# A gated attention block with a routed expert layer: rows copied a chunk later, another order at the handover, row loads one tile further ahead

## The chip, the core and the metric

One core of a Trainium2 chip. The metric is the device time of one execution in microseconds; the times shown are a median over several runs. The core has five engines that run their own instruction streams and signal each other by semaphores: PE (matmuls), ACT (activations, which need a function table loaded), DVE (elementwise work, scans, statistics), POOL (elementwise work and the indirect DMAs), and SP, which here only issues DMAs. All tensors are float32.

## The reference

x has 32 sequences of 256 rows of 128 numbers (8192 rows). Cut to what matters:

```
mod = silu(c) @ wmod                       # six vectors for each sequence
h   = layernorm(x) * (1 + ca) + sa
K   = exp(h Wk1 + bk1);  S = cumsum(K * h) / (cumsum(K) + 1e-6)
Q   = sigmoid(h Wq1 + bq1);  O_ar = S * Q
E   = h[1:] - O_ar[:-1];  K2 = sigmoid(0.02 * (h Wk2 + bk2) / sqrt(128))
O_ma = cumsum(K2 * E) * q2(Q)              # the "moving average" part
x1  = x + ga * ((O_ar + O_ma) Wproj + bproj)
z   = layernorm(x1) * (1 + cb) + sb
e   = argmax(z @ centroids.T)              # one of 8 experts for each row
out = x1 + gb * (z + relu(norm_e(z) W1[e] + b1[e]) W2[e] + b2[e])
```

## The kernel before, in words

**Chunk stage.** The rows are taken in 16 chunks of two sequences (512 rows). The loops of all engines run over c, and one pass holds parts of several chunks: x of chunk c+3 is transposed (PE, L806) and scaled on the way out of PSUM ("turned x", ACT `turned_x`, L953); exp, tanh of k2 and tanh of q (ACT L970, L974, L979) and DVE's scans make O_ar and O_ma; PE adds both products into x1's bank (L779, and L796 for the moving average). ACT copies x1 to `rows` (`sum_of`, L925). Of x1 DVE takes statistics, ACT makes rstd (`rstd_of`, L945 and L947, in the loop L1021 and L1031), POOL makes zz (L501), PE transposes it (`turn_z`, L700), ACT scales it ("turned z", `turned_z`, L933), and PE computes the logits from it (L723) and transposes it back (L700). ACT copies that result to `rows` (`rows_of`, L939: "rows copy"). POOL scatters each finished chunk of rows by expert into DRAM (L538, four indirect DMAs a chunk). Ln and Exp use other tables than tanh, so ACT loads a table twice a pass (L960, L965) and once more in the last pass (L996).

The order on each engine is written out by hand. In ACT's pass c, with z = c-3, it is: turned x, `sum_of(c-1)`, `turned_z(z)`, Ln, table, Exp, exp of k, `rows_of(z)`, tanh, tanh. PE's turn of z waits for ACT's turned x, since both use one bank. In the last pass (c = 15) ACT takes x1's copy, then the table load and `rstd_of(13)`, then `turned_z(12)`; PE runs `turn_z(13)` ahead of the last moving-average products.

**Tile stage.** When 10 chunks are scattered and a first plan is made, SP starts to load tiles of 256 rows that belong to one expert: 25 tiles, 0 to 24, the first 13 from the first plan, tile 13 and on only after all chunks are scattered. Then 11 tiles, 25 to 35, follow in blocks of 128 rows with an expert for each (the last has one block). A tile goes: row load (SP), statistics (DVE `tile_stats`, L1141, for tile j+3), rstd (ACT), normalising (DVE L1485), transposing (PE L843), scaling (ACT), hidden matmuls (PE L830, in block tiles L834), relu (ACT, and for the last quarter of a block tile DVE L1494), the second matmul (PE L858), three sums and a product (DVE, last L1706), store (POOL L613).

SP's queue in step i: the W1 load of tile i+1 (waits until tile i-2's hidden matmuls are done), the row load of tile i+3 (waits for the stores' sums `b_u` and POOL's `b_ids` of the tile whose buffer it takes, nine tiles before), and, in the block stage, two W1 loads of tile i+2. In the block stage a row load is two DMAs of 192.5 KB, and W1 two DMAs of 256 KB.

Of the kernel before, what the change touches and what calls it, by code (L numbers as in the profile page):

```python
# [24 lines left out]
def build_block(nc, x, Wq1, bq1, Wk1, bk1, Wk2, bk2, Wproj, bproj, centroids, ln_g, ln_b,  # L25
# [8 lines left out]
    NC = T // CT  # L34
# [34 lines left out]
    with ExitStack() as ctx:  # L69
# [203 lines left out]
        def in_a(c):  # L273
            return 0 <= c < NC

        def in_b(j):
            return 0 <= j < NJ
# [70 lines left out]
        def _(sp):  # L348
# [43 lines left out]
            for c in range(NC + 1):  # L392
                if in_a(c):
                    fill(c)
                m = c + 7
# [21 lines left out]
            for k in range(RR):  # L417
                sp.wait_ge(s_scat[k], 16 * CN * len(range(k, G1 * GT // CN, RR)))
            sp.wait_ge(s_planned, 1)
            for i in range(-3, NJ):  # L420
                w, m = i + 1, i + 3
                if 0 <= w < NF:
                    e = sp.value_load(plan[0:1, w, 0:1], min_val=0, max_val=E - 1)
                    wait(sp, b_l1, FC * (w - WR + 1))
                    sp.dma_start(w1_full[:, w % WR, :], W1[bass.ds(e, 1), :, :].rearrange("o d f -> (o d) f")
                                 ).then_inc(s_w1[w % WR], 16)
                if in_b(m):
                    if m == N1:
                        for k in range(RR):
                            sp.wait_ge(s_scat[k], 16 * CN * (NC // RR))  # L430
                        sp.wait_ge(s_planned, 2)
                    if m == NF:
                        sp.wait_ge(s_planned, 4)
                    if m < IN_X:

                        sp.wait_ge(s_proj, NC - XR + ((m + 1) * FS * RW - 1) // (CN * D) + 1)
                    wait(sp, b_u, m - FR + 1)
                    wait(sp, b_ids, m - FR + 1)
                    if m < NF:
                        r = sp.value_load(plan[0:1, m, 1:2], min_val=0, max_val=E * RS)  # L440
                        sp.dma_start(full(m), rows_dram[bass.ds(r, FT), :]
                                     .rearrange("(s p) w -> p s w", p=P)).then_inc(s_full[m % FR], 16)
                    else:
                        for t in parts(m):
                            r = sp.value_load(plan[0:1, entry(m, t), 1:2], min_val=0, max_val=E * RS)
                            sp.dma_start(full(m)[:, t, :], rows_dram[bass.ds(r, P), :]).then_inc(s_full[m % FR], 16)
                v = i + 2
                if NF <= v < NJ:
                    wait(sp, b_l1, FC * (v - WR + 1))
                    for t in parts(v):  # L450
                        e = sp.value_load(plan[0:1, entry(v, t), 0:1], min_val=0, max_val=E - 1)
                        sp.dma_start(w1_of(v, t), W1[bass.ds(e, 1), :, :].rearrange("o d f -> (o d) f")
                                     ).then_inc(s_w1[v % WR], 16)
# [182 lines left out]
        def _(pe):  # L636
# [120 lines left out]
            for c in range(-3, NC):  # L757
# [29 lines left out]
                    keep_going(8, ps_t)  # L787
                if in_a(q) and q > 0:
                    queries(q)
                if c == NC - 1:  # L790
                    turn_z(NC - 3)
                if in_a(c):
                    pe.wait_ge(s_M, c + 1)
                    for t in range(CN):
                        s, l = t * P // L, t * P % L
                        mm = pe.matmul(ps_proj[:, t * P:(t + 1) * P], Mp[:, c % 2, s, l:l + P], wg[:, CS * c + s, :],  # L796
                                       start=False, stop=(t == CN - 1))
                    mm.then_inc(s_proj, 1)
                if in_a(a):
                    wait(pe, s_hT, 2 * a)  # L800
                    wait(pe, s_h2T, 2 * max(0, z + 1))
                    for t in range(CN):

                        if a == 0 or t == 0:
                            pe.wait_ge(s_xh, CN * a + t + 1 if a == 0 else CN * (a + 1))
                        mm = pe.transpose(ps_t[:, t * P:(t + 1) * P], xh[:, a % 2, t, :], ident[:, :])  # L806
                    mm.then_inc(s_xT, 1)
# [58 lines left out]
            pe.wait_ge(s_experts, 16 * FC)  # L866
            pe.wait_ge(s_planned, 1)

            keep_going(6, ps_q)
            turn_tile(0)  # L870
            logits(NC - 3)
            turn_back(NC - 3)
# [33 lines left out]
        def _(act):  # L906
# [84 lines left out]
            for c in range(-2, NC):  # L991
                n, q, z, y, o = c + 2, c + 1, c - 3, c - 2, c - 1
                i = c + 4
                if c == NC - 1:
                    sum_of(o)
                    act.preload_act_table_set("natural_log_exp_and_others")  # L996
                    rstd_of(NC - 3)
                if in_a(n) and n != 1:
                    turned_x(n)
                if c == -2:  # L1000
# [7 lines left out]
                                   scale=2.0).then_inc(s_abs, 1)  # L1008
                if in_a(o) and c < NC - 1:
                    sum_of(o)  # L1010
                if in_a(z):
                    turned_z(z)
                if in_a(q):
                    logs(q)
                kinds = slice(0 if in_a(i) else 1, 2 if in_a(y) else 1)
# [19 lines left out]
                if c == NC - 1:  # L1035

                    act.wait_ge(s_planned, 1)
                    of_first = [expert_of(act, n) for n in range(2)]
                if in_a(z):
                    rows_of(z)  # L1040
                if c == 9:
                    act.wait_ge(s_parp, 1)
# [39 lines left out]

            of_blocks = []
            act.wait_ge(s_par, 1)
            rstd_of_tile(0)
            turned_z(NC - 3)
            rstd_of_tile(1)
            experts = [norm_of_expert(0)]
            rstd_of(NC - 2)
            sum_of(NC - 1)  # L1090
            experts.append(norm_of_expert(1))
            rows_of(NC - 3)
# [653 lines left out]
```

## Time and profile before

| | us |
|---|---|
| median of 3 runs (lowest, highest) | 332.16 (331.11, 333.01) |
| the profiled execution | 329.52 |
| its span, first to last instruction | 327.7 |
| busy: PE, PE weight loads | 287.7, 233.1 |
| busy: DVE, ACT, POOL | 253.1, 245.9, 235.4 |

Mean granted PE clock 0.978 of 2.4 GHz. In the page's 40 slices PE is at 9 tenths through the tile stage, and ACT and DVE are at 9 tenths through most of the chunk stage. Busy time is an average over stages with different limits: which wait ends last in a stage has to be read from its timeline. In timeline rows the first column is the start in us from the span's start, the second the duration of the (merged) entry; square brackets give the idle time before it and who ended it.

### The profile page before, as it was taken

What the parts mean: (1) busy time and instruction counts of PE and PEld (TensorE: products, weight loads), DVE (VectorE), ACT (ScalarE), POOL (GpSimd) and SP (SyncE); (2) the same over time, 40 slices, a digit from 0 to 9 for tenths busy, and PEclk for the clock granted to TensorE, in tenths of its full rate; (3) what the DMA queues carried; (4) which work ended last, traced back from release to release, by engine and by line L of the source; (5) the groups of instructions that cost most, each with busy time, mean ns of one, the idle gap of its engine ahead of it and who ended that gap; (6) DMA issues with size and microseconds to landing.
All of it is one profiled execution on the core that took longest, in us unless ns stands there. A gap on an engine that the chain in (4) does not pass through costs nothing.

```text
span 327.7 us, 7878 instructions
## 1 busy us (share of the span) xinstructions
PE 287.7 (88%) x1911; PEld 233.1 (71%) x1911; DVE 253.1 (77%) x653; ACT 245.9 (75%) x538; POOL 235.4 (72%) x371
## 2 busy tenths in 40 slices
PE   8777888899989898998899999999999998998920
PEld 7544445666666565665688999999999998988920
DVE  4898998999999998999945577986666656675840
ACT  2878989999999999999667567776777775666500
POOL 7985476578889888888548878788888753545670
PEclk9999999999999999999989999999999999999985
DMA  7332288626479976444568899778787777877100
GB/s 213 99 105 90 72 228 248 161 90 225 137 202 198 253 196 188 100 149 160 177 224 266 235 289 331 252 219 232 217 228 229 208 225 239 233 220 239 34 16 0
DMA packets 49426, 60.84 MB, mean 186 GB/s; under 512 B 5557, under 2 KB 38095, under 8 KB 49379
## 3 DMA queue, kind: packets, MB, share of 16 engines
q1 hardware_dynamic: 42806, 43.11, 48.9%
q0 software_dynamic: 6368, 16.82, 14.0%
q10 hardware_dynamic: 208, 0.41, 0.4%
q8 instruction: 17, 0.28, 0.3%
q14 instruction: 27, 0.22, 0.2%
HBM read 39.90 MB, written 20.87 MB: 185 GB/s over the span
## 4 chain that ended last, share of the span: by engine, by line
PE 51%; ACT 26%; issue 8%; DVE 7%; SPq 3%; DMA 1%; POOL 1%; POOLq 0%; DVEq 0%; ACTq 0%
PE bank L858 17%; PE bank L830 13%; ACT L965 4%; ACT L960 4%; PE bank L834 4%; PE bank L700 3%; ACT shared L953 3%; ACT shared L960 2%; ACT shared L965 2%; ACT h2T L933 2%; PE bank L843 2%; ACT bank L974 2%; PE bank L796 2%; ACT bank L970 2%; ACT bank L979 2%
## 5 line engine op out<-in xcount | busy, mean ns | idle before, releaser
L613 POOL DMA_INDIRECT out_dram<-shared,ids x71 | 72.4, 1020 | 36.1 <-DVE shared L1706 18.3
L538 POOL DMA_INDIRECT expert_rows<-rows,slots x64 | 66.7, 1043 | 15.8 <-issue 15.0
L858 PE MATMUL bank<-w_all,shared 128*128 x568 | 69.3, 275 | 0.1
L858 PEld LDWEIGHTS bank<-w_all,shared 128*128 128x128 f32 x568 | 66.2, 192 | 0.4 <-issue 0.3
L1054 ACT ACTIVATE shared<-bank,par 128x256 f32<-128x256 f32 x100 | 40.9, 472 | 18.3 <-PE bank L830 18.0
L830 PE MATMUL bank<-shared,early 128*128 128x256 f32 x200 | 47.9, 382 | 0.0
L501 POOL TENSOR_SCALAR zz<-rows,negm,rstd 128x128 f32<-128x128 f32 x64 | 32.3, 517 | 18.6 <-ACT rstd L1031 11.0
L830 PEld LDWEIGHTS bank<-shared,early 128*128 128x128 f32 x200 | 36.1, 190 | 4.1
L1511 DVE TENSOR_TENSOR shared<-bank,b_bc 128x256 f32<-128x256 f32 (+1 forms) x42 | 14.7, 366 | 25.9 <-PE bank L858 24.9
L493 POOL TENSOR_SCALAR xh<-x_in,negm,rstd 128x128 f32<-128x128 f32 x64 | 28.8, 461 | 5.3 <-DVE negm L1260 3.9
L1077 ACT ACTIVATE shared<-bank,par 128x256 f32<-128x256 f32 (+1 forms) x46 | 22.7, 515 | 8.7 <-PE bank L843 6.6
L834 PE MATMUL bank<-shared,rows 128*128 128x128 f32 x168 | 22.1, 279 | 3.9 <-DVE shared L1494 3.9
L1061 ACT ACTIVATE shared<-bank,par 128x128 f32<-128x128 f32 x64 | 18.8, 370 | 8.2 <-PE bank L834 8.1
L834 PEld LDWEIGHTS bank<-shared,rows 128*128 128x128 f32 x168 | 20.1, 192 | 5.0 <-DVE shared L1494 5.0
L796 PEld LDWEIGHTS bank<-wg,Mp 128*128 128x128 f32 x128 | 17.6, 200 | 7.2 <-issue 7.2
L965 ACT ACT_TABLE_LOAD x16 | 20.5, 1283 | 0.3
L960 ACT ACT_TABLE_LOAD x16 | 20.5, 1283 | 0.3
L766 PE MATMUL bank<-x_in,ident 128*128 128x512 f32 x32 | 17.1, 615 | 4.1 <-ACT rows L925 3.2
L933 ACT ACTIVATE h2T<-bank,mod 128x256 f32<-128x256 f32 x32 | 16.3, 559 | 5.3 <-PE bank L700 5.3
L700 PE MATMUL bank<-ident,zz 128*128 128x128 f32 x64 | 10.5, 289 | 11.1 <-ACT shared L953 10.3
L1197 DVE TENSOR_TENSOR_SCAN shared<-seq_mask,bank 128x512 f32<-128x512 f32 x16 | 19.4, 1211 | 0.3 <-ACT bank L970 0.3
L1209 DVE TENSOR_TENSOR_SCAN shared<-seq_mask,bank 128x512 f32<-128x512 f32 x16 | 19.3, 1209 | 0.1
(216 smaller groups left out, 659.5 us busy)
## 6 DMA issues: line engine op xcount, KB each, us to landing
early<-in_L_ffn_W_dram SPq DMA_DIRECT2D x25, 256.0 KB
x_in<-expert_rows SPq DMA_DIRECT2D x15, 385.0 KB, 4.7
rows<-in_L_ffn_W_dram SPq DMA_DIRECT2D x21, 256.0 KB
x_in<-in_L_attn_x_dram SPq DMA_DIRECT2D x16, 256.0 KB, 3.4
rows<-gates_rows SPq DMA_DIRECT2D x32, 128.0 KB, 5.4
full<-expert_rows SPq DMA_DIRECT2D x10, 385.0 KB, 4.5
expert_rows<-pad_rows SPq DMA_DIRECT2D x9, 385.0 KB, 8.4
full<-expert_rows SPq DMA_DIRECT2D x11, 192.5 KB, 3.1
```

The lines of the kernel that those rows point to most:

```text
L493: pool.tensor_scalar(xh[:, a % 2, t, :], x_in[:, a % XR, t, :], negm[:, a, 0, t:t + 1], rstd[:, a, 0, t:t + 1], ALU.add, ALU.mult).then_in ...
L501: pool.tensor_scalar(zz[:, y % 2, t, :], rows[:, y % RR, t, W:W + D], negm[:, y + 6, 1, t:t + 1], rstd[:, y + 6, 1, t:t + 1], ALU.add, ALU ...
L538: pool.indirect_dma_start(rows_dram, bass.IndirectOffsetOnAxis(ap=slots[:, c * CN + t:c * CN + t + 1], axis=0), rows[:, c % RR, t, :], Non ...
L613: pool.indirect_dma_start(out_rows, bass.IndirectOffsetOnAxis(ap=ids[:, u % IR, t:t + 1], axis=0), u_sb[:, k, t, :], None, bounds_check=T - 1,
L796: mm = pe.matmul(ps_proj[:, t * P:(t + 1) * P], Mp[:, c % 2, s, l:l + P], wg[:, CS * c + s, :], start=False, stop=(t == CN - 1))
L830: mm = pe.matmul(hidden_at(j, f), w1_of(j, 0)[:, f * P:(f + 1) * P], zT[:, j % 2, :], start=True, stop=True)
L834: mm = pe.matmul(hidden_at(j, f)[:, t * P:(t + 1) * P], w1_of(j, t)[:, f * P:(f + 1) * P], zT[:, j % 2, t * P:(t + 1) * P], start=True, st ...
L858: mm = pe.matmul(out_at(o, t), hid[:, k, f, t * P:(t + 1) * P], of_expert(w2_all, e, f * D, (f + 1) * D), start=(f == 0), stop=(f == FC - 1))
L933: act.activation(h2T[:, z % 2, s * L:(s + 1) * L], src[:, s * L:(s + 1) * L], ACT.Identity, bias=mod[:, 2, z * CS + s:z * CS + s + 1], sca ...
L960: act.activation(lnK[:, q % 2, :, :], Kc[:, :, :], ACT.Ln, scale=LN_SCALE, bias=epsk[:, :]).then_inc(s_ln, 1)
L965: act.activation(lnK[:, q % 2, :, :], lnK[:, q % 2, :, :], ACT.Exp, scale=-1.0, bias=lnbias[:, :]).then_inc(s_R, 1)
L1054: r = act.activation(hid[:, j % 2, f, :], hidden_at(j, f), ACT.Relu, bias=par[:, 2 + f, bass.ds(e, 1)])
```

## The change

On ACT the rows copy of chunk z moves from the end of pass c to the next pass, between x1's copy and the turned z; the copy of chunk 12 stays where it was. In pass 15 the table load and `rstd_of(13)` move behind `turned_z(12)`. After the loop `rstd_of(14)` and the rstd of tiles 0 and 1 come first, then `turned_z(13)`. On PE the last moving-average products come ahead of `turn_z(13)`, and the filler transposes after the loop are four instead of six. SP's row loads run one tile further ahead from step 7 on, with two in step 6.

```diff
@@ sync
+            def rows_in_step(i):
+                ms = (i + 3,) if i < 6 else (i + 3, i + 4) if i == 6 else (i + 4,)
+                return [m for m in ms if in_b(m)]
             for i in range(-3, NJ):
-                w, m = i + 1, i + 3
+                w = i + 1
                 if 0 <= w < NF:
...
-                if in_b(m):
+                for m in rows_in_step(i):
@@ tensor, loop over c
-                if c == NC - 1:
-                    turn_z(NC - 3)
                 if in_a(c):
                     pe.wait_ge(s_M, c + 1)
...
                     mm.then_inc(s_proj, 1)
+                if c == NC - 1:
+                    turn_z(NC - 3)
@@ tensor, after the loop
-            keep_going(6, ps_q)
+            keep_going(4, ps_q)
@@ scalar, loop over c
                 if c == NC - 1:
                     sum_of(o)
-                    act.preload_act_table_set("natural_log_exp_and_others")
-                    rstd_of(NC - 3)
...
+                if in_a(z - 1):
+                    rows_of(z - 1)
                 if in_a(z):
                     turned_z(z)
+                if c == NC - 1:
+                    act.preload_act_table_set("natural_log_exp_and_others")
+                    rstd_of(NC - 3)
...
-                if in_a(z):
+                if c == NC - 1:
                     rows_of(z)
@@ scalar, after the loop
             act.wait_ge(s_par, 1)
+            rstd_of(NC - 2)
             rstd_of_tile(0)
+            rstd_of_tile(1)
             turned_z(NC - 3)
-            rstd_of_tile(1)
             experts = [norm_of_expert(0)]
-            rstd_of(NC - 2)
             sum_of(NC - 1)
```

## Rows read from the trace of the kernel before

**Rows 1.** Timeline, ACT, one chunk of the chunk stage.

```profile
112.13 0.60 ACT L925 ACTIVATE rows<-bank 128x512 f32<-128x512 f32 x1
113.05 1.02 ACT L933 ACTIVATE h2T<-bank,mod 128x256 f32<-128x256 f32 x2 [0.32 <-PE bank L700]
...
118.90 0.59 ACT L939 ACTIVATE rows<-bank 128x512 f32<-128x512 f32 x1
119.38 0.66 ACT L974 ACTIVATE bank<-bank,bias 128x512 f32<-128x512 f32 x1
119.95 0.67 ACT L979 ACTIVATE bank<-bank,bias 128x512 f32<-128x512 f32 x1
120.54 1.02 ACT L953 ACTIVATE shared<-bank,mod 128x256 f32<-128x256 f32 x2
```

**Rows 2.** Timeline, PE, same chunk: first logits weight load, last x transpose.

```profile
114.15 0.19 PEld L723 LDWEIGHTS bank<-centT,h2T 128*128 128x128 f32 x1 [0.23 <-ACT h2T L933]
...
120.23 0.27 PE L806 MATMUL bank<-ident,xh 128*128 128x128 f32 x1
```

**Rows 3.** Timeline, ACT, pass c = 15.

```profile
157.59 0.60 ACT L925 ACTIVATE rows<-bank 128x512 f32<-128x512 f32 x1 [0.23 <-PE bank L796]
158.21 1.28 ACT L996 ACT_TABLE_LOAD   x1
...
159.95 1.00 ACT L933 ACTIVATE h2T<-bank,mod 128x256 f32<-128x256 f32 x2
```

**Rows 4.** Timeline, PE, from pass c = 15 to the first tile.

```profile
158.10 0.63 PE L700 MATMUL bank<-ident,zz 128*128 128x128 f32 x4
...
161.01 1.06 PE L723 MATMUL bank<-centT,h2T 128*128 128x8 f32 x8 [1.09 <-ACT h2T L933]
...
164.48 1.92 PE L796 MATMUL bank<-wg,Mp 128*128 128x128 f32 x8
...
168.66 1.89 PE L830 MATMUL bank<-shared,early 128*128 128x256 f32 x8
```

**Rows 5.** Timeline, POOL (zz of chunks 13 and 14) and DVE, same stretch.

```profile
160.14 1.73 POOL L501 TENSOR_SCALAR zz<-rows,negm,rstd 128x128 f32<-128x128 f32 x4 [2.85 <-ACT rstd L947]
...
161.83 0.67 DVE L1249 SCALAR_TENSOR_TENSOR Mp<-bank,shared 128x512 f32<-128x512 f32 x1
...
168.85 1.74 POOL L501 TENSOR_SCALAR zz<-rows,negm,rstd 128x128 f32<-128x128 f32 x4 [4.31 <-ACT rstd L947]
```

**Rows 6.** Windows: us, busy of PE, PEld, DVE, ACT, POOL (count), clock, DMA, GB/s.

```profile
164.00:166.00 2.00, 2.00 (x12) 2.00 (x11) 0.36 (x2) 1.24 (x4) 0.54 (x2) 0.50 0.80 265
```

**Rows 7.** Windows, hidden matmuls of tile 26 to those of 27.

```profile
270.39:274.18 3.79, 3.79 (x37) 3.79 (x35) 1.47 (x6) 2.66 (x10) 1.49 (x2) 1.00 0.83 239
```

**Rows 8.** Timeline, SP's queue, tail: W1 of tile 32, rows of tile 35.

```profile
291.26 0.34 SPq L452 DMA_DIRECT2D rows<-in_L_ffn_W_dram  x1
...
296.90 0.34 SPq L446 DMA_DIRECT2D full<-expert_rows  x1
```

**Rows 9.** Timeline, DVE, statistics of tile 35.

```profile
301.29 0.43 DVE L1141 BATCH_NORM_STATS2 bbn<-full 128x6 f32<-128x256 f32 x1 [2.01 <-DMA full<-expert_rows]
```

**Rows 10.** Source view of L446, the row blocks' loads: issue to landing.

```profile
DMA to landing us min/median/max: 2.8/3.1/4.4
```

**Rows 11.** Timeline, PE, hidden matmuls of tile 34.

```profile
306.16 1.95 PE L834 MATMUL bank<-shared,rows 128*128 128x128 f32 x16
```

**Rows 12.** Timeline, POOL, first store of tile 32 and the last store.

```profile
310.43 0.99 POOL L613 DMA_INDIRECT out_dram<-shared,ids  x1 [0.16 <-issue]
...
318.35 0.97 POOL L613 DMA_INDIRECT out_dram<-shared,ids  x1 [0.30 <-issue]
```

**Rows 13.** Timeline, SP's queue, row load of tile 13.

```profile
206.83 0.38 SPq L441 DMA_DIRECT2D x_in<-expert_rows  x1
```

**Rows 14.** Waits of SP's queue, 196 to 212 us: total, times, longest.

```profile
SPq L430 <- DMA expert_rows<-rows,slots: 0.6, 1, 0.6
```

**Rows 15.** Timeline, PE, hidden matmuls of tile 11.

```profile
213.98 1.89 PE L830 MATMUL bank<-shared,early 128*128 128x256 f32 x8
```

## The prediction

> **What bounds the kernel now.** I read the chain of waits first. It shows two long stretches. In the chunk stage (about 26 to 158 us) it goes to and fro between PE and ACT once in every chunk. In the tile stage (about 168 us on) it is PE alone, until 274 us, where it hops to DVE, SP's queue and one row load. So I then opened the timelines: one chunk, the handover between the stages, and the tail.
>
> One chunk, ACT [rows 1]: x1's copy (L925) starts at 112.13, the turned z (L933) at 113.05 after 0.32 us of waiting for PE's transposes, the rows copy (L939) at 118.90, the tanh of q (L979) at 119.95, and the next chunk's turned x (L953) at 120.54. PE, same chunk [rows 2]: the logits' weight load waits 0.23 us for ACT's turned z and starts at 114.15, 0.08 us after L933 ends (113.05 + 1.02 = 114.07). From there PE runs without a gap to its last x transpose at 120.23, and L953 starts 0.31 us behind that (0.27 us of matmul and 0.04 of signal). The loop that sets a chunk's time is thus: turned x, z's transposes, turned z, PE's run, turned x. ACT's own path ends in the same moment: L974 to L979 is 0.57, and 119.95 + 0.57 = 120.52 against 120.54. The two tie within 0.02 us. An ACT made shorter gains nothing by itself; a turned z that starts later costs in full.
>
> The handover: ACT copies x1 of chunk 14 at 157.59, loads the table 158.21 to 159.49, and only then turns z of chunk 12, at 159.95 [rows 3]. PE transposed that z at 158.10 and idles 1.09 us before the logits at 161.01. The eight moving-average products of the last chunk start at 164.48 and take 1.92 us; the first tile's hidden matmuls start at 168.66 [rows 4]. Their input was made by DVE by 162.50 (161.83 + 0.67) [rows 5]: they wait only for their place in PE's order. From 164 to 166 us the granted clock is 0.50, the 1.2 GHz level [rows 6].
>
> The tail: an undisturbed tile of blocks is 3.79 us, all of it PE [rows 7]. SP issues four DMAs a tile (two row blocks, two W1 blocks). From the second W1 block of tile 32 (291.26) to the row block of tile 35 (296.90) there are five gaps, 1.13 us each [rows 8], so 4.51 us a tile: SP is slower than PE. DVE then sits 2.01 us for those last rows [rows 9] with relu, sums and the normalising behind it in its order, and PE waits for DVE.
>
> **The rows copy a chunk later (ACT).** Nothing added: 16 copies before and after. From 118.90 it moves behind x1's copy. ACT there has 0.92 us from 112.13 to 113.05. Two copies need 0.50 (L925's 0.60 less an overlap of 0.10, as L939's 0.59 has: 118.90 to 119.38 is 0.48) + 0.48 = 0.98, so the turned z starts at 113.11 instead of 113.05: +0.06 a chunk. The 0.48 saved later is only waiting for PE. Nine chunks (4 to 12, those with a rows copy there and this loop): +0.55 us. Bounds: if ACT and not PE held the loop, the 0.32 of wait goes: 9 x -0.32 = -2.9; if a copy costs 0.17 more than in [rows 1], 9 x 0.16 = +1.5. I take +0.55, since the 0.31 us and the 0.23 us wait [rows 2] both say PE. What waits for the rows copy: PE's turning back (after the logits, over 1 us later) and POOL's scatter, which in POOL's order stands a whole chunk behind the copy even then. Free.
>
> **The handover (ACT, PE, POOL).** After x1's copy at 157.59 come the rows copy (158.09 to 158.67) and z, whose transposes end at 158.73 (158.10 + 0.63): turned z at 158.76 to 159.76. PE's logits can start at 159.92 (161.01 less its idle 1.09). Logits, turning back and the eight first products, at full clock 0.92 + 0.47 + 0.89 (0.11 or 0.12 for each matmul pass), end at 162.20; the moving-average products wait for DVE's 162.50 and take about 0.96 (half of the 1.92 at half clock) to 163.5, against 166.4 before. The table load now starts at 159.78, 1.57 later, so POOL's zz of chunk 13 goes from 160.14 to 161.71 and ends at 163.44 [rows 5]: just in time for PE, which reaches its transposes at 163.5. Behind it POOL idled 4.31 us before zz of chunk 14 [rows 5], so the 1.57 are covered there, and that zz too comes earlier (its rstd is now first after the loop). Then: transposes to 164.15, turned z to 165.2, logits and turning back 1.4 to 166.7, two tile transposes 0.2, hidden matmuls at 166.9. Before: 168.66. Term: -1.75. The two dropped fillers are worth 0.1 each beside a wait. Bounds: 0 (another wait of the same length) and -2.9 (all that the products gain, 166.4 to 163.5). The rstd of tile 1 now stands before the turned z of chunk 13 and waits for row load 1 through DVE's statistics. Queued behind it are that z, the first expert's scaling and the x1 copy, and PE waits for all three; a load that lands after 164.15 would eat into the term, down to the bound of 0.
>
> [Rows 3] show the table load begin 0.02 us after the copy ends and the turned z stand two small activations behind it, with no room for more. The Trainium skill, "ScalarE: Activation LUTs", section "What ACT_TABLE_LOAD costs", counts a drain of about 1.38 us to each load, 2.66 in all; this trace disagrees. By the page, zz of chunk 13 and all behind it would be 1.38 later, and the time 1.38 above what I forecast; I give that 1 in 100, inside case C.
>
> **Row loads one tile further ahead (SP).** No DMA is added; from step 7 each row load is issued a step earlier, with two at step 6. In the tail each row block is issued 4.51 us sooner; DVE's wait was 2.01, so no tile waits for rows. What is late next is W1. The extra row load was issued long before the tail, so W1's second block of tile v keeps its slot: 291.26 for tile 32, 4.51 less for each tile before. Those of 33 and 34 come 1.1 and 2.3 sooner. Their landing is not shown; a row block of 192.5 KB takes 2.8 to 4.4, median 3.1 [rows 10]; for 256 KB I take 3.6. Then hidden 32 starts at max(274.18 + 5 x 3.79 = 293.13, 291.26 + 3.6 = 294.86) = 294.86, and hidden 34 at 294.86 + 7.58 = 302.44 against 306.16 [rows 11]. PE: -3.7. The end hangs on POOL's stores, in one unbroken row from tile 32 (310.43) to the last (318.35), 7.92 us [rows 12]. The first of them stands 4.27 us behind the start of hidden 34, as its sums need that long, so the row moves with PE: 302.44 + 4.27 + 7.92 = 314.63, term -3.7. Bounds: landing 2.8: hidden 34 at 301.64, -4.5; 4.4: 303.24, -2.9; no W1 wait at all: 274.18 + 7 x 3.79 = 300.71, -5.4; and 0 if W1 takes the whole place.
>
> SP passes one danger. The load of tile 13 stands behind a wait for all scatters, over at 206.83 - 0.6 or so [rows 13, 14]. It now stands before W1 of tile 11 (so far ahead of it), which slips to 206.83 + 1.13 = 207.96; that tile's matmuls start at 213.98 [rows 15], a lead of 6.0 against at most 4.4 for a load [rows 10]. Free with 1.6 us to spare. Between steps 13 and 17 the row loads also reach the point where they wait for POOL's ids; W1 slips by up to 3 us of a lead of 9. Free.
>
> **Sum.** +0.55 - 1.75 - 3.7 = -4.9. The profiled execution took 329.52 (span 327.7, 1.8 lie around it), so 324.6; the median shown is 332.16, 2.64 above it, and the same saving gives 327.3.
>
> **Rivals.**
> - A: ACT really holds the chunk loop. For it: the tie of 0.02 us. Against: 0.31 us behind PE's last transpose. -2.9 in place of +0.55: 323.8. Chance 0.11.
> - C: PE's clock falls at the handover anyway. For: it was down at 164 to 166 [rows 6], soon after PE's idle 1.09 us, and PE still has short waits there. Against: that idle goes, and in the chunk stage PE waits each chunk without a fall. The products, transposes and fillers between 162.5 and 164.7 at half speed cost about 1 of the 1.75: 328.3. Chance 0.14. The Trainium skill, "TensorE: Matmul & The Clock Gate", section "Part 1: The HAM clock gate", says the clock follows how busy PE has lately been, which speaks for no fall.
> - W: W1 takes most of the rows' place. At 5.4 us of landing (1.0 above the longest row load) hidden 34 starts at 304.24 and the tail gives -1.9: 329.1. For: SP issues slower than PE eats. Chance 0.14.
> - N: the row loads do not do what they say, since the same 4.51 us of SP a tile remain: only handover and chunks, -1.2: 331.0. Against: their slots move up in a count of issues. Chance 0.05.
> - S, slower than before: SP stands at the scatter wait of tile 13, and W1 of tile 11 comes after PE wants it. Each us that the scatters land later than 206.2 + 1.6 is a us of PE; it decides against the change from 4.9 us beyond that, and with 8 us it is 335.3. Against: [rows 14] show 0.6 us of wait. Chance 0.04.
>
> **Numbers.** The forecast, 327.3, has the remaining 0.52. The range 323.4 to 330.2 holds it with its bounds, C, W and over half of A; left out are N, S and the rest of A. What can be told from no change here is 0.5%, 1.66 us: faster means below 330.5. Faster 0.91 (forecast, A, C, W), same 0.05 (N), slower 0.04 (S).
>
> **What would show it.** In the profile after: from turned z to turned z 0.06 us more a chunk and no wait of ACT before it (A: 0.3 less). The table load behind the turned z of chunk 12; moving-average products of chunk 15 near 163 at clock 1.0, hidden matmuls of tile 0 some 1.75 sooner. W1 of tile 11 behind the load of tile 13 and no PE wait at tile 11. In the tail no DVE wait for row loads; what stands there instead, PE waiting for W1, sizes W. I am wrong if PE's tail tiles stay near 4.5 us, or if a wait of SP reaches PE between 206 and 235 us.

## The result, and the profile after

| | us | ratio to the kernel before, 95% interval |
|---|---|---|
| kernel before, 4 runs | 331.63 (329.99 to 333.01) | |
| changed kernel, 4 runs | 326.03 (324.01 to 327.96) | 0.9885 [0.984, 0.993] |
| third set of runs, below: before, 17 runs | 330.13 | |
| changed kernel there, 6 runs | 327.35 | 0.9884 [0.9827, 0.9941] |

Faster by 1.15% by the ratio, about 3.8 us, with an interval of 2.3 to 5.3 us. The two medians, of four runs each, stand 5.6 us apart in the first pair and, of 17 and 6 runs, 2.8 us in the third set, so these few runs give the gain to a microsecond or two and no better. The forecast was 4.9 less, 327.3; it lies inside the interval. The profiled execution took 325.93, its span is 324.1 (327.7 before) and its mean clock 0.978, as before.

Starts in us, from the timelines of both kernels (each line's difference holds what came before it):

| | before | after | difference |
|---|---|---|---|
| PE transposes z of chunk 12 | 158.10 | 160.31 | +2.21 |
| hidden matmuls of tile 0 | 168.66 | 169.47 | +0.81 |
| of tile 2 | 178.02 | 178.12 | +0.10 |
| of tile 25 | 266.60 | 266.46 | -0.14 |
| of tile 34 | 306.16 | 302.90 | -3.26 |
| end of the span | 327.7 | 324.1 | -3.6 |

Of the +2.21, 1.8 are not the change's: the first chunks start that much later in this execution, in code that the diff leaves alone. The other 0.4 came in between, over the 12 chunks from the turn of z of chunk 0 (46.55 before, 48.36 after). Other profiles show both starts for both kernels (the turn of z of chunk 12 is at 160.45 in a second profile of the kernel before, at 158.38 in a second one of the changed kernel). So lengths are compared here, not positions.

**Chunk loop.** Timeline of ACT in the changed kernel, one chunk (answers [rows 1]; L958 is turned x, L930 x1's copy, L944 the rows copy, L938 turned z):

```profile
122.50 1.02 ACT L958 ACTIVATE shared<-bank,mod 128x256 f32<-128x256 f32 x2 [0.37 <-PE bank L811]
123.41 0.60 ACT L930 ACTIVATE rows<-bank 128x512 f32<-128x512 f32 x1
123.89 0.60 ACT L944 ACTIVATE rows<-bank 128x512 f32<-128x512 f32 x1
124.37 1.04 ACT L938 ACTIVATE h2T<-bank,mod 128x256 f32<-128x256 f32 x2
...
131.84 1.02 ACT L958 ACTIVATE shared<-bank,mod 128x256 f32<-128x256 f32 x2 [0.37 <-PE bank L811]
```

The wait before the turned z is gone, and a wait of 0.37 for PE's x transposes stands before the turned x instead. From turned x to turned x it is 9.34, against 9.32 before. ACT's saving turned into waiting: PE's run holds this loop, with ACT's stretch from turned x to turned z in it.

**Handover.** Timeline of PE in the changed kernel (answers [rows 4]; L705 turns z, L728 logits, L799 moving-average products, L645 fillers, L848 transposes of tile 0, L835 its hidden matmuls):

```profile
160.31 0.66 PE L705 MATMUL bank<-ident,zz 128*128 128x128 f32 x4
...
162.08 1.06 PE L728 MATMUL bank<-centT,h2T 128*128 128x8 f32 x8
...
164.62 1.16 PE L799 MATMUL bank<-wg,Mp 128*128 128x128 f32 x8
165.78 0.66 PE L705 MATMUL bank<-ident,zz 128*128 128x128 f32 x4
166.27 0.60 PE L645 MATMUL bank<-ident 128*128 128x128 f32 x4
167.24 0.44 PE L848 MATMUL bank<-ident,shared 128*128 128x128 f32 x2 [0.37 <-DVE shared L1494]
167.86 1.06 PE L728 MATMUL bank<-centT,h2T 128*128 128x8 f32 x8 [0.18 <-ACT h2T L938]
...
169.47 1.89 PE L835 MATMUL bank<-shared,early 128*128 128x256 f32 x8
```

Windows of the same kernel (us, busy of PE, PEld, DVE, ACT, POOL with counts, granted clock, DMA share, GB/s; answers [rows 6]):

```profile
164.00:166.00 2.00, 1.90 (x15) 1.52 (x14) 1.55 (x4) 0.94 (x4) 1.85 (x5) 1.00 0.85 261
```

What PE waited for in the two short gaps between 164 and 166 us (DVE's input of the moving-average products; POOL's zz of chunk 13):

```profile
163.88 0.68 DVE L1258 SCALAR_TENSOR_TENSOR Mp<-bank,shared 128x512 f32<-128x512 f32 x1
163.98 1.75 POOL L506 TENSOR_SCALAR zz<-rows,negm,rstd 128x128 f32<-128x128 f32 x4 [3.58 <-ACT rstd L952]
```

PE's products start at 164.62, 0.06 behind DVE's end (163.88 + 0.68), and its turn of z of chunk 13 at 165.78, 0.05 behind POOL's (163.98 + 1.75). The idle 1.09 before the logits is gone, and the clock is 1.00 where it was 0.50. From turn to tile 0 it is 9.16 instead of 10.56, from turn to tile 2 17.81 instead of 19.92. ACT shows a new wait (answers [rows 3]; L1020 is the table load):

```profile
161.01 1.02 ACT L938 ACTIVATE h2T<-bank,mod 128x256 f32<-128x256 f32 x2 [0.27 <-PE bank L705]
162.04 1.28 ACT L1020 ACT_TABLE_LOAD   x1
163.34 0.30 ACT L950 ACTIVATE lnv<-bn,epsv 128x4 f32<-128x4 f32 x1
163.67 0.21 ACT L952 ACTIVATE rstd<-lnv 128x4 f32<-128x4 f32 x1
165.03 0.60 ACT L944 ACTIVATE rows<-bank 128x512 f32<-128x512 f32 x1 [1.16 <-issue]
...
166.80 1.00 ACT L938 ACTIVATE h2T<-bank,mod 128x256 f32<-128x256 f32 x2
```

Between 163.88 and 165.03 ACT reads the first two experts from the plan into registers. The last row is the turned z of chunk 13: it has no wait, for ACT comes to it only at 166.80, 0.36 after PE's transposes have ended (165.78 + 0.66 = 166.44). The load starts 0.01 us after the turned z ends (161.01 + 1.02 = 162.03), and the next activation 0.02 after the load. The Trainium skill, "ScalarE: Activation LUTs", section "What ACT_TABLE_LOAD costs", adds a drain of about 1.38 us to a load; this second place shows no room for one either.

**Tail.** Hidden matmuls of tiles 30 to 34, timeline of PE in the changed kernel (answers [rows 11]):

```profile
285.42 2.02 PE L839 MATMUL bank<-shared,rows 128*128 128x128 f32 x16
...
290.26 2.02 PE L839 MATMUL bank<-shared,rows 128*128 128x128 f32 x16 [0.81 <-issue]
...
294.53 2.02 PE L839 MATMUL bank<-shared,rows 128*128 128x128 f32 x16 [0.24 <-issue]
...
299.04 2.02 PE L839 MATMUL bank<-shared,rows 128*128 128x128 f32 x16 [0.48 <-issue]
...
302.90 1.95 PE L839 MATMUL bank<-shared,rows 128*128 128x128 f32 x16
```

SP's queue there (second W1 block of tiles 31, 32 and 33; answers [rows 8]), and the source view of L457, the W1 blocks' loads (its last line; it stands beside [rows 10]):

```profile
286.98 0.34 SPq L457 DMA_DIRECT2D rows<-in_L_ffn_W_dram  x1
...
291.46 0.34 SPq L457 DMA_DIRECT2D rows<-in_L_ffn_W_dram  x1
...
294.89 0.34 SPq L457 DMA_DIRECT2D rows<-in_L_ffn_W_dram  x1
```

```profile
DMA to landing us min/median/max: 2.8/3.0/3.3
```

The hidden matmuls start 3.28, 3.07 and 4.15 us behind the issue of the second W1 block of their tile, after short waits to which the profile gives no releaser ("issue"). The landing is on record for only 7 of the 21 W1 blocks, and the last line is over those 7. One is the second block of tile 32: issued at 291.46 with 2.98 to landing, it was there at 294.44, and PE starts at 294.53. For tile 33 no landing is on record, and 4.15 is longer than any of the 7. That this wait too is W1's is an argument by elimination: the tile's turned rows were ready at 297.75 (ACT, 296.94 + 0.81) and the first relus of tile 32, which free the bank, were done by 297.01 (ACT, 295.86 + 1.15), both long before 299.04. Tiles 25 to 30 pass at 3.79 or 3.80. From tile 25 to 34 it is 36.44 instead of 39.56. DVE's waits for row loads from 264 us on fall from 13.5 us in 9 to 4.0 in 4, and no wait of PE for DVE is left there (3.9 us in 6 before). The last store (answers the second of [rows 12]):

```profile
314.76 0.97 POOL L618 DMA_INDIRECT out_dram<-shared,ids  x1 [0.30 <-issue]
```

It is 3.59 earlier, 0.33 more than the start of tile 34; the stores moved with PE.

### The profile page after: what moved, and what is told of

Its sections match the earlier page's. It is cut to its first block, busy times and chain, and to the rows that moved or that the text cites. A ratio compares the mean times of both kernels' runs of the same rounds, so it can differ in the third digit from the quotient of the medians.

```text
span 324.1 us, 7874 instructions
## 1 busy us (share of the span) xinstructions
PE 286.6 (88%) x1909; PEld 232.0 (72%) x1909; DVE 253.1 (78%) x653; ACT 244.6 (75%) x538; POOL 238.4 (74%) x371
## 4 chain that ended last, share of the span: by engine, by line
PE 56%; POOL 23%; issue 10%; ACT 3%; DMA 3%; DVE 1%; POOLq 1%; ACTq 0%; DVEq 0%
PE bank L863 18%; PE bank L835 14%; POOL expert_rows L543 9%; PE bank L839 6%; POOL xh L498 6%; POOL zz L506 5%; PE bank L848 2%; PE bank L771 2%; PE bank L784 2%; PE bank L705 2%; PE bank L728 2%; PE bank L799 2%; PE bank L759 2%; PE bank L756 2%; PE bank L749 1%
## 5 line engine op out<-in xcount | busy, mean ns | idle before, releaser
L618 POOL DMA_INDIRECT out_dram<-shared,ids x71 | 73.2, 1031 | 31.0 <-issue 12.8
L835 PE MATMUL bank<-shared,early 128*128 128x256 f32 x200 | 47.7, 381 | 0.0
L835 PEld LDWEIGHTS bank<-shared,early 128*128 128x128 f32 x200 | 36.1, 190 | 4.1
L498 POOL TENSOR_SCALAR xh<-x_in,negm,rstd 128x128 f32<-128x128 f32 x64 | 29.5, 472 | 4.3 <-DVE negm L1269 3.9
L839 PE MATMUL bank<-shared,rows 128*128 128x128 f32 x168 | 20.9, 277 | 1.5 <-issue 1.5
L799 PEld LDWEIGHTS bank<-wg,Mp 128*128 128x128 f32 x128 | 16.7, 191 | 7.5 <-issue 7.2
L705 PE MATMUL bank<-ident,zz 128*128 128x128 f32 x64 | 10.1, 280 | 12.1 <-ACT shared L958 10.3
L958 ACT ACTIVATE shared<-bank,mod 128x256 f32<-128x256 f32 x32 | 16.3, 561 | 5.8 <-PE bank L811 5.8
## 6 DMA issues: line engine op xcount, KB each, us to landing
full<-expert_rows SPq DMA_DIRECT2D x11, 192.5 KB, 3.0
```

What stands on the lines that cost most here:

```text
L498: pool.tensor_scalar(xh[:, a % 2, t, :], x_in[:, a % XR, t, :], negm[:, a, 0, t:t + 1], rstd[:, a, 0, t:t + 1], ALU.add, ALU.mult).then_in ...
L618: pool.indirect_dma_start(out_rows, bass.IndirectOffsetOnAxis(ap=ids[:, u % IR, t:t + 1], axis=0), u_sb[:, k, t, :], None, bounds_check=T - 1,
L835: mm = pe.matmul(hidden_at(j, f), w1_of(j, 0)[:, f * P:(f + 1) * P], zT[:, j % 2, :], start=True, stop=True)
L839: mm = pe.matmul(hidden_at(j, f)[:, t * P:(t + 1) * P], w1_of(j, t)[:, f * P:(f + 1) * P], zT[:, j % 2, t * P:(t + 1) * P], start=True, st ...
```

## The experiments

Three sets, each on one chip, every kernel beside the kernel before. The chips differed: the kernel before took 359.72 us (35 runs) in the first set, 366.97 (23 runs) in the second and 330.13 (17 runs) in the third. That matters below.

### One part at a time

`rows_ahead_only` is the kernel before with SP's part of the diff, `handover_only` with ACT's and PE's edits of the last pass and behind the loop, `rows_copy_only` with the moved rows copy, each as in the diff above. `after_again` is the changed kernel.

> The kernel before with SP's row loads one tile further ahead and nothing else. Theory (the tail is set by when SP issues; W1 is late next): hidden matmuls of tile 25 at the same place relative to tile 0, those of tile 34 3.0 to 3.7 us nearer to those of tile 25 than the 39.6 us of before, whole kernel 3.3 us faster (2.5 to 4.0). No DVE wait for row loads over 1.5 us in the tail; PE instead waits a few tenths of a us for W1 in tiles 31 to 33. Rival N (SP spends the same time a tile, so nothing is won): within 0.5 us of before. Rival S: a PE wait at tile 11 or 12, since W1 of tile 11 now stands behind SP's wait for the scatters.

360.02, ratio 0.9964 [0.9911, 1.0017].

> The kernel before with only the handover in the new order (turned z of chunk 12 ahead of the table load, moving-average products ahead of the turn of chunk 13, rstd first after the loop, four fillers). Theory: from PE's turn of chunk 12 to the hidden matmuls of tile 0 9.2 us instead of 10.56, granted clock 1.0 between 162 and 168 us of the span, tail as before; whole kernel 1.4 us faster (1.0 to 2.3; the upper end if tiles 0 to 2 also close up). Rival C (the clock falls in the handover anyway): 0.4 us faster. Rival (POOL's later zz of chunk 13 pushes the scatters and SP's first wait): no gain.

360.6, ratio 1.0026 [0.9986, 1.0066].

> The kernel before with only the rows copy moved a chunk later. Theory (PE holds the chunk loop): from turned z to turned z 0.02 to 0.06 us more a chunk, so 0 to 0.6 us slower over all, ACT idle about 0.4 us a chunk before the turned x instead of before the turned z. Rival A (ACT holds the loop): 0.3 us less a chunk, 2.9 us faster.

360.97, ratio 1.0045 [1.0005, 1.0084].

> The changed kernel itself, on the same chip as its three parts. Theory: the parts add, 0.3 - 1.4 - 3.3 = -4.4 us (-3.5 to -5.6). Rival: they overlap (the tail's gain depends on when the tile stage begins), and the whole is smaller than the sum by more than 1 us.

358.83, ratio 0.996 [0.9921, 0.9998].

By the times, nothing but the whole and the copy differs from the kernel before. The copy is slower by 0.2 to 3.0 us (0 to 0.6 expected). The handover's interval, -0.5 to +2.4 us, leaves out the 1.4 that were expected of it, and the row loads' is -3.2 to +0.6 (3.3 expected). The whole gains 1.4 us, not 4.4, with an interval that overlaps the first one (0.9921 to 0.9998 against 0.984 to 0.993). Windows of `handover_only` and, for comparison, of the changed kernel in the third set (`after_third`), in the tile stage (in `handover_only` the hidden matmuls of tiles 3 to 6 lie between 188 and 217 us):

```profile
188.00:192.00 4.00, 1.76 (x5) 1.28 (x6) 0.00 (x0) 1.40 (x3) 2.32 (x4) 0.50 0.62 190
...
208.00:216.00 8.00, 0.00 (x0) 0.00 (x0) 0.24 (x2) 1.22 (x4) 6.42 (x9) 0.51 0.37 116
```

```profile
188.00:192.00 4.00, 4.00 (x35) 3.68 (x35) 3.60 (x17) 1.77 (x6) 3.08 (x4) 1.00 0.86 283
```

And the waits of `handover_only` between 176 and 216 us (total, times, longest):

```profile
ACT shared L1055 <- remote: 18.5, 4, 6.4
DVE shared L1512 <- remote: 12.6, 3, 8.0
```

One engine's wait is up to 8 us long, with no releaser on this core, and PE, DVE and ACT stand still together for up to 4.1 us here (from 208.4) and up to 4.8 in `w1_by_act`. POOL works on meanwhile: 6.42 of the 8 us in the last window. All eight profiles of the first two sets have such waits ("remote") between 176 and 225 us, none of the six others has one there, and the changed kernel is in both groups, so the edits alone do not bring it. (The kernel before was profiled only on a chip without such waits.) What it is the profile doesn't say, and I leave it open. Parts worth 1 to 3 us drown in it: the tail from tile 25 to 34 is 40.48 in `rows_ahead_only`. What such a profile still shows is what lies ahead of its first stall. There `rows_copy_only` has 9.35 a chunk with the wait of 0.37 before turned x, and `handover_only` 9.14 from turn to tile 0 at clock 1.00.

### What limits now

`w1_by_act` is the changed kernel, with ACT issuing the second W1 block of each block tile. `w1_by_act_old_rows` does it in the kernel before.

```diff
@@ sync
-                    for t in parts(v):
+                    for t in range(1):
@@ scalar, in tile j
+                v = j + 2
+                if NF <= v < NJ and len(parts(v)) == 2:
+                    act.wait_ge(b_l1, FC * (v - WR + 1))
+                    act.dma_start(w1_of(v, 1), W1[bass.ds(of_blocks[FS * (v - NF) + 1], 1), :, :]
+                                  .rearrange("o d f -> (o d) f")).then_inc(s_w1[v % WR], 16)
```

> The changed kernel, but in the tiles of blocks the second W1 block of each tile is issued by ACT, behind its relus, and not by SP. Theory (after the change SP's 4 issues of 1.12 us a tile against PE's 3.79 set the tail, through W1): SP has 3 issues a tile, 3.4 us, PE no longer waits for W1, hidden matmuls of tile 34 start 34.1 us after those of tile 25 instead of 36.4, whole kernel about 2 us faster than the changed one. Rival (ACT's issue costs as much as SP's, 1.1 us, and ACT has 1.1 us to spare a tile): PE waits for ACT's relus instead, gain under 0.5 us or a loss.

360.91, ratio 0.9815 [0.9758, 0.9872] to the kernel before. The changed kernel was not run on this chip, so whether it is 2 us faster than that one is not told here; tile 25 to 34 is 38.35 in a profile with stalls, where 34.1 was expected.

> The kernel before with only that edit (row loads at their old distance, ACT issues the second W1 block). Theory (the late rows of the tail were SP's backlog and not the distance as such): with 3 issues a tile SP has no backlog, rows are in time at the old distance too, tile 25 to 34 in 34.1 to 35 us instead of 39.6, 4 to 5 us faster than before. Rival (the distance of one tile itself is what helps): DVE still waits for row loads in most tail tiles, 25 to 34 over 37 us.

365.2, ratio 0.9942 [0.9909, 0.9975]: 2.1 us faster, half of the 4 to 5 expected. Tile 25 to 34 is 38.19, which is the rival's "over 37", but on such a chip; DVE still waits 6.5 us in 6 for row loads from 288 us on. So taking an issue off SP helps at the old distance too, and does not by itself bring the rows in time.

`x1_first` puts x1's copy ahead of turned x on ACT, and on PE the x add ahead of z's turn and the O_ar products ahead of the logits. `experts_read_late` moves ACT's two register reads behind the loop, between the rstd of tile 1 and the turned z of chunk 13:

```diff
-                    act.wait_ge(s_planned, 1)
-                    of_first = [expert_of(act, n) for n in range(2)]
@@ behind the loop, after the two tiles' rstd, ahead of turned_z
+            act.wait_ge(s_planned, 1)
+            of_first = [expert_of(act, n) for n in range(2)]
```

> The changed kernel with another order in the chunk loop: ACT copies x1 before the turned x; PE adds x to x1's bank while it waits for that, and computes the O_ar products between z's transposes and the logits. Theory (PE's run behind the turned z holds the loop, ACT has 0.37 us a chunk to spare): PE's run is 0.9 us shorter, then ACT holds the loop at 9.0 us instead of 9.34, nine chunks, 3 us faster (2 to 3.5). Rival (DVE, 8.9 us busy a chunk, holds the loop, or the O_ar product is late): within 0.5 us of the changed kernel.

367.31, ratio 1.0026 [0.9982, 1.007] to the kernel before; the changed kernel was not run beside it. As that one was never slower than the kernel before, the 3 us expected did not come. Timeline of ACT in `x1_first`, one chunk:

```profile
123.82 0.60 ACT L930 ACTIVATE rows<-bank 128x512 f32<-128x512 f32 x1
124.30 1.03 ACT L958 ACTIVATE shared<-bank,mod 128x256 f32<-128x256 f32 x2
125.20 0.63 ACT L944 ACTIVATE rows<-bank 128x512 f32<-128x512 f32 x1
126.55 1.02 ACT L938 ACTIVATE h2T<-bank,mod 128x256 f32<-128x256 f32 x2 [0.72 <-issue]
```

The chunk takes 9.73 instead of 9.34. Turned x no longer waits, so ACT holds the loop now, and it has a new idle 0.72 before turned z: z's transposes stand behind the x add on PE, which needs x1's copy. Without the 0.72 the chunk would be the 9.0 that was expected (9.73 - 0.72). The wait was moved ahead of the wrong product.

> The changed kernel with ACT's two reads of the first tiles' experts moved from behind rstd of chunk 13 to behind the rstd of tile 1. Theory (those reads, 1.16 us of ACT without an activation, make the first tile's rstd late, and PE waits 0.37 us for that tile): handover 9.16 to 8.8 us, 0.3 us faster. Rival (the reads now stand before the turned z of chunk 13 and delay that): no gain or up to 0.5 us slower.

364.14, ratio 0.9876 [0.9824, 0.9929] to the kernel before; again the changed kernel was not run beside it. The 1.16 us wait is gone (the rows copy starts at 163.44 instead of 165.03, in a profile in which all of this is 0.34 us earlier), but from turn to tile 0 it is 9.58 instead of 9.12 to 9.16. ACT and PE in that stretch:

```profile
165.48 0.20 ACT L994 ACTIVATE brstd<-blnv 128x2 f32<-128x2 f32 x1
166.87 1.02 ACT L938 ACTIVATE h2T<-bank,mod 128x256 f32<-128x256 f32 x2 [1.19 <-PE bank L705]
```

```profile
165.42 0.66 PE L705 MATMUL bank<-ident,zz 128*128 128x128 f32 x4
...
167.95 1.06 PE L728 MATMUL bank<-centT,h2T 128*128 128x8 f32 x8 [1.21 <-issue]
```

The profile puts the 1.19 down to PE, but PE's transposes ended at 166.08 (165.42 + 0.66), 0.79 before ACT starts. What fills the time from 165.68 on is the two reads, as long here as in their old place. So the rival came true: the reads delay the turned z of chunk 13, and PE waits 1.21 for it instead of 0.37 and 0.18. The reads are on the path in both places. In the kernel before they cost nothing, since ACT waited 1.64 us for PE there. With the 0.79 off, this profile would have the 8.8 us that were expected (an estimate, 9.58 - 0.79); a place for the reads where ACT is idle was not tried.

### On a chip without the stalls

> The kernel before, unchanged, looked at on the same chip as the three that follow. In the profiles of the earlier experiments, whose kernel before took 360 to 367 us and not 332, all engines stood still together several times between 172 and 216 us, where this one in its first profile ran through. Theory 1 (the chip's doing, whatever the kernel): if this chip too takes 355 us or more for this kernel, the profile has these stalls, hidden 3 starts at 187 us or later instead of 183, and the tail from hidden 25 to hidden 34 is over 39.6 us. Rival (the stalls come with the edits): this profile shows none whatever the time, hidden 3 at 183. If the chip takes about 332 us, neither is told apart and the three that follow are read against 332.

329.59, span 327.8. The chip took 330.13 for this kernel, so as the text on record says, stalls or no stalls on a slow chip were not told apart by it. It told something else. PE in this profile of the kernel before:

```profile
160.45 0.63 PE L700 MATMUL bank<-ident,zz 128*128 128x128 f32 x4
...
163.36 1.06 PE L723 MATMUL bank<-centT,h2T 128*128 128x8 f32 x8 [1.09 <-ACT h2T L933]
...
166.07 1.06 PE L796 MATMUL bank<-wg,Mp 128*128 128x128 f32 x8
...
169.37 1.89 PE L830 MATMUL bank<-shared,early 128*128 128x256 f32 x8
```

```profile
164.00:166.00 2.00, 2.00 (x20) 2.00 (x20) 1.70 (x5) 0.98 (x3) 1.54 (x3) 1.00 0.98 293
```

The same order, the same idle 1.09, but the clock stays at 1.00, and from turn to tile 0 it is 8.92 us, 0.2 less than in the changed kernel. Over all profiles, with the clock of the two-microsecond window in which it was lowest:

| order at the handover | profiles | turn of z 12 to tile 0 | to tile 2 | lowest clock |
|---|---|---|---|---|
| old, clock fell | before, rows_ahead_only, rows_ahead_again | 10.56, 10.42, 10.41 | 19.92, 19.77, 19.75 | 0.50, 0.50, 0.51 |
| old, clock fell, with the moved copy | rows_copy_only | 10.89 | 20.26 | 0.50 |
| old, clock held | before_look, w1_by_act_old_rows | 8.92, 8.89 | 18.26, 18.01 | 1.00 |
| new, clock held | after, handover_only, after_again, w1_by_act, w1_by_act_again, x1_first | 9.12 to 9.16 | 17.66 to 17.81 | 1.00 |
| new, experts' reads late | experts_read_late | 9.58 | 18.12 | 1.00 |
| new, clock fell | after_third | 11.21 | 20.74 | 0.55 |

(In `w1_by_act_old_rows` a stall had come before, at 151.6, and the clock had fallen to 0.50 at 156 to 162 us.) Four of six against one of eight are too few executions to say how often either order loses the clock; what the table shows is what a fall costs. In `after_third` tile 1's rows landed late, and DVE waited for them with tile 0's normalising queued behind:

```profile
165.35 0.43 DVE L1150 BATCH_NORM_STATS2 bbn<-x_in 128x6 f32<-128x256 f32 x1 [2.38 <-DMA x_in<-expert_rows]
```

PE was busy 0.93 and 1.12 of 2 us in the two windows from 164 to 168, and the clock stood at 0.55 and 0.60 in the next two.

> The changed kernel, unchanged. Theory (handover 1.4 us shorter, tail 3.1 us, chunk loop unmoved): 4 to 6 us less than the kernel before on this chip, ratio 0.984 to 0.990, and the handover from the turned z of chunk 12 to hidden 0 at 9.16 us. Rival (on a chip with engine-wide stalls in the tile stage the tail's gain goes under in them): ratio 0.994 to 0.998.

327.35, ratio 0.9884 [0.9827, 0.9941]: the first result again, although its profile has the bad handover. Tile 25 to 34 is 36.50.

> The kernel before with the row loads' order alone, again. Theory (the tail's part of the gain is all the row loads'): 3 to 4 us less than the kernel before, hidden 25 to 34 as in the changed kernel, handover 10.5 us as before. Rival (row loads by themselves do little, as 0.996 in the first comparison said): under 1.5 us less.

327.86 (12 runs), ratio 0.9919 [0.9882, 0.9957], so 2.7 of the 3.8 us. Tile 25 to 34 is 37.00, against 39.25 in `before_look`. The theory's 3 to 4 was a little too much. One stop of PE is 1.73 us long, before tile 32. Its row, and the source view of L457 for the one W1 block issued at 292.10, the tile's second:

```profile
296.32 2.02 PE L839 MATMUL bank<-shared,rows 128*128 128x128 f32 x16 [1.73 <-issue]
```

```profile
DMA to landing us min/median/max: 4.1/4.1/4.1
```

292.10 + 4.13 = 296.23, and PE starts 0.09 later: the stop is W1, which took 1.2 us longer to land than the median of this profile (2.9).

> The changed kernel, with ScalarE issuing the second W1 block of every block tile, again beside the changed kernel itself this time. Theory (after the change SyncE's queue and with it W1 is what the tail waits for): 1 to 4 us less than the changed kernel, hidden 25 to 34 in 34.5 to 36 us where the chip has no stalls, no wait of TensorE for W1 over 0.3 us. Rival (TensorE's own work with ScalarE's copies sets the tail by now, and the issue costs ScalarE what SyncE saves): same as the changed kernel within 0.5 us.

324.76 (6 runs), ratio 0.9821 [0.9773, 0.9869]. The median is 2.6 below the changed kernel's and five of the six runs lie below five of its six, but the intervals overlap: likely faster, not shown. Hidden matmuls of tiles 26, 27, 28 and 31:

```profile
271.74 1.95 PE L839 MATMUL bank<-shared,rows 128*128 128x128 f32 x16
...
277.45 2.02 PE L839 MATMUL bank<-shared,rows 128*128 128x128 f32 x16 [1.76 <-issue]
...
281.32 1.95 PE L839 MATMUL bank<-shared,rows 128*128 128x128 f32 x16
...
292.69 1.95 PE L839 MATMUL bank<-shared,rows 128*128 128x128 f32 x16
```

From tile 27 on every tile takes 3.68 to 3.87, where `after_third` spends 0.58, 0.33, 0.75 and 0.64 us above 3.79 on its tiles 29 to 32. Those 2.3 us of waits for W1 are gone when SP issues three DMAs a tile: ACT's block is issued 4.7 us ahead of its tile (280.43 for tile 29, against 285.11). But the expectation, 34.5 to 36 us and no wait for W1 over 0.3, missed: from tile 25 to 34 it is 36.37, no better than 36.44 and 36.50, because of the stop of 1.76 us before tile 27. The profile gives it no releaser either, and it has the look of a late W1 block: ACT's block of that tile was issued at 270.85, and the three landings on record around it (issued 262.75, 266.69 and 274.43) took 4.8, 4.3 and 4.9 us. Its own landing is not on record, so this is not shown. The median of this kernel is the lowest of all.

## Why the prediction was right, step by step

- **Who bounds the chunk loop: right.** PE. The turned z has no wait, the turned x has 0.37, the period grew. Rival A is refuted: the saved 0.48 of ACT came back as waiting. `x1_first` shows the other side, that ACT is close behind: a wait of 0.72 on it cost 0.39 a chunk.
- **Rows copy, +0.06 a chunk: mis-sized, harmless.** Measured +0.02 to +0.03 a chunk; from the turn of z of chunk 0 to that of chunk 12 the profiles of kernels with the moved copy and the old loop order take 111.9 to 112.0 us, those without it 111.5 to 111.7 (but for the one with a stall), so +0.2 to +0.5 in all, against +0.55. (The upper bound has a slip: a copy dearer by 0.17 makes 0.06 + 0.17 a chunk, 2.1 us and not 1.5.) The cause: from L930 to L938 it is 0.96 with both copies between them, where 0.98 was counted against 0.92 before.
- **Handover, -1.75: the size is near by luck, the reason only half right.** The first pair of profiles has -1.40 to tile 0 and -2.11 to tile 2. But with the clock held, the old order needs 8.9 us to tile 0 and the new one 9.1; to tile 2 the new one is 0.2 to 0.6 shorter. Nearly all of the first pair's step is thus the clock, which the old order lost at this place in four of six profiles and the new one in one of eight. The working put about 1 us of the step down to the clock (rival C) and the rest to the earlier turned z. That rest did not come. PE starts the logits 1.14 sooner after its turn of z than in `before_look` (1.77 against 2.91), and gives this back in small gaps: 0.51 in the two sets of products (1.15 and 1.16 from start to start, against 0.90 each), where it waits for DVE's input and POOL's zz, and 0.7 from the fillers to the logits of chunk 13 (1.59 against 0.87, with two fillers fewer), where it waits for DVE's tile 0 and for a turned z that stands behind the two reads, a copy and three rstd on ACT. The first pair of gaps was in the working (DVE's 162.50, POOL's 163.44 "just in time"). The reads were not: they are 1.16 us of ACT that the prediction put at nothing. By its working tile 0 starts 8.80 after the turn of z of chunk 12 (158.10 to 166.9); measured is 9.16, and 0.36 is also by how much ACT's turned z comes behind PE's transposes, where the working had it right behind them. Rival C was given 0.14 as a fall that goes on; it happened in one of eight.
- **The danger named there was real.** "A load that lands after 164.15 would eat into the term": in `after_third` tile 1's rows landed at 165.3 and DVE held tile 0 for 2.38 us. The predicted path, rstd of tile 1 ahead of turned z, is one of two; the other is DVE's own order.
- **Row loads, -3.7 for tile 34: right in kind, 0.6 too large.** Measured -3.12 from tile 25 to 34, and -2.8 against the second profile of before. DVE still waits 4.0 us for rows, where no wait was said, but rows are no longer what PE waits for; W1 is, as said. W1's slots came as worked out (second block of tile 32 at 291.46, 291.26 said). Tile 32 started at 294.53 (294.86 said, with a landing of 3.6; it is 3.0, max 3.3). The step that failed is "hidden 34 at 294.86 + 7.58": tile 33 took 4.51 after tile 32, not 3.79, as it waited again: it started 4.15 after the issue of its W1 block, and the working had 3.6 for a landing. So one fixed landing time was the weak point; the landings on record run from 2.6 to 4.9. Rivals W (-1.9) and N (0) are below what the rows show; `rows_ahead_again` gives 2.7 of the time to the row loads alone.
- **Rival S: did not happen.** No wait of PE from 200 to 235 us; tile 11 started at 213.84, before at 213.98.
- **The sum.** -4.9 said, -3.8 by the ratio: the times do not tell the two apart (2.3 to 5.3). The traces say which terms are off: the tail's by 0.6 to 0.9, and the handover's -2.1 is there only against executions in which the old order loses the clock. `before_look`, which starts as late as the first profile of the changed kernel and holds its clock, is 3.7 us longer than it: 0.4 to tile 2, 2.8 in the tail, 0.3 behind it. How much hangs on the clock shows in the time from the turn of z of chunk 0 to the end of the span: 281.2 and 278.8 us in the two profiles of the kernel before, 275.8 and 279.4 in the two of the changed one. That a single pair came out near the forecast is in part luck. The handover's part by itself was timed only on a chip with stalls, where it gained nothing, so its share of the 3.8 stays open.

## What to carry to other kernels

When a stage ends in a wait for a load, look at the whole queue that issues it, not at the load: moving the row loads ahead handed the wait to W1 in the same queue, and taking an issue off that queue removed most of those waits. A load then needs a lead that covers its slow landings, not its median. A gain at a place where the clock was low has to be split into clock and order, and one profile can't do that: take several of the kernel before. Work taken off the engine that only ties with the bound comes back as waiting. When instructions change place on an engine, count its register reads with them: a profile shows them only as idle time, and can put them down to another engine.

## What the runs showed of the hardware

- The clock can fall or hold at the same place with the same 1.09 us of idle before it: with the old order it was at 1.2 GHz (0.50 and 0.51) in some executions and 2.4 GHz in others, and that alone is 1.5 to 1.7 us from turn to tile 0. The Trainium skill, "TensorE: Matmul & The Clock Gate", section "Part 1: The HAM clock gate", says of the warm-up that the monitor's window runs free, so that the same kernel can come out differently from run to run. The two profiles of the kernel before agree that it can; this is in the middle of a kernel, and the reason is not shown here.
- Two register reads of the plan by ACT took 1.16 us (1.19 in their other place); an issue of SP with its register load takes 1.1 (286.98 after 285.86), so four a tile are 4.5 against PE's 3.79.
- A W1 block of 256 KB landed in 2.8 to 3.3 us in the first profile of the changed kernel, no later than a row block of 192.5 KB (2.8 to 4.4 in [rows 10]). Only 7 of its 21 landings are on record; in `rows_ahead_again` one took 4.1, and in `w1_by_act_again` they run from 2.6 to 4.9.
- The same program took 330, 360 and 367 us on three chips, with mean clocks of the whole span of 0.974, 0.948 and 0.938. On the latter two PE, DVE and ACT stood still together for up to 4.8 us at a time in the stretch from 176 to 225 us, in every profile taken there (all of edited kernels; the kernel before was not profiled there). The same change gave 0.9884 on the first and 0.996 on the second, with intervals that overlap.
